# Moving the message sums between two sets of picks, and the addition of x behind the variance

## The chip, the cores and the metric

The kernel runs on one core of a Trainium2 chip. The metric is the device time in microseconds (us) of one execution. Inside the core five engines work from queues of their own and meet only at semaphores: TensorE (PE in the profile; PEld is its loading of weights), VectorE (DVE), ScalarE (ACT), GpSimd (POOL) and SyncE (SP), the last of which only issues transfers here.

## The reference

One layer of a graph network with a residual, on 100000 nodes of 96 numbers and 25000 edges whose target `dst` is sorted:

```python
h = jnp.maximum(_layernorm(x, axis=-1), 0.0)
concat = jnp.concatenate([h[src], h[dst], edge_attr], axis=-1)      # 25000 x 256
gates = jax.nn.sigmoid(concat @ W_e + b_e)
messages = jax.nn.softplus(concat @ W_n + b_n)
h_new = jax.ops.segment_sum(gates * messages, dst, num_segments=n)
edge_count = jnp.clip(segment_sum(ones, dst), 1.0, None)[:, None]
out = x + (h + h_new / edge_count)
```

## The kernel before

All five engines run the same loop of 49 steps (and a few steps of run-in and run-out), each with its own order of work written out by hand in a function `step(i)`. A step handles 2048 rows of x (16 rows in each of 128 partitions, "node rows") and 512 edges (4 tiles of 128). The engines work at different depths: in step i, DVE makes the statistics of node chunk i + 3, ACT and DVE normalize chunk i + 2, TensorE picks from chunk d = i + 1, edges k = i - 1 are transposed and multiplied, edges j = i - 2 go through the activations, and edges m = i - 3 are summed by target.

- TensorE, `step(i)` from L992. It first makes the **first set of picks** (`picks(d, 0, at)`, L1016): the rows of h that the sorted edges need are selected from node_out by multiplying with one-hot columns, 8 blocks, into the one tile `pick_ps` (L976). Their places come from 16 registers loaded at L967. It then transposes the gathered source rows (L1021) and the edge attributes (L1026), makes the **second set of picks** (L1030, again L976, with another register load), the **sums** (`sums(m)`, L1032, with L988 and L989: messages of equal target are added by a 0/1 matrix), and the final products of edges k (L1041 to L1043). Each set of picks waits for `pick_out`, ACT's copy of the set before out of `pick_ps`. The sums wait for `message_done`, `same_done` and `final_done`; the final products wait among others for `trans_out` and `attr_out`, ACT's copies of the transposes.
- ACT, `step(i)` from L498: sigmoid (L492), normalization of the gathered source rows (L508), the copy of the first picks into dst_t (L496), four node rows (L478), the copies of the transposes (L526, L528), the copy of the second picks (L496 again), then node rows mixed with the three activations of edges j (L540, L545, L550) and the logarithm and exponential of the variance (L484, L488). The last L478 of a step raises `node_norm_done`, for which the first picks of the next step wait.
- DVE, `step(i)` from L784: Newton steps for 1/sigma (L755 to L770), its share of node rows (L801, L806), the 0/1 matrices (L746, L749), the message (L739), statistics of node rows (L717), one-hot columns (L777), then **the addition of x** to the 16 normalized node rows of chunk d (L821, one operation over 128 x 1536, after both sets of picks have read them: it waits for `pick_done` 2d + 2), the statistics of the gathered rows (L826), counts (L722), inverse counts, `final` (L731) and the variance (L833 to L847), and the last two operations on the logarithms (L858, L861), which wait for ACT's L550.
- SP waits for L821 (`node_sum_done`) before it loads the next chunk of x (L304) and stores the finished one to out.
- POOL gathers source rows of x (L397) and adds `final` to rows of out (L411), four indirect transfers of each kind in a step. The latter wait for `final_done` and for the store of the chunk.

Of the kernel before, what the change touches and what calls it, by code (L numbers as in the profile page):

```python
# [52 lines left out]
def build(nc, x, src, dst, edge_attr, w_e, b_e, w_n, b_n, out, count_table, dst_pad, low_pad):  # L53
    ctx = ExitStack()
    with ctx:
# [544 lines left out]
        def _(dve):  # L600
# [183 lines left out]
            def step(i):  # L784
# [29 lines left out]
                for g in (0, 1) if i == -2 else (i + 3,):  # L814
                    if 0 < i + 3 and g < GROUPS:
                        one_hot(g)
                if runs_step(d):
                    wait(dve, node_norm_done, d + 1)
                    wait(dve, dve_norm_done, d + 1)
                    wait(dve, pick_done, 2 * d + 2)  # L820
                    nc.vector.tensor_tensor(node_out[d % NS][:, :, :], node_out[d % NS][:, :, :], node_x[d % NS][:, :, :],  # L821
                                            ALU.add).then_inc(node_sum_done, 1)
                if runs_step(i):
                    dve.wait_ge(gathered[i % NS], 16 * TB * (i // NS + 1))
                    for r in range(TB):
# [19 lines left out]
                if runs_rows(i):  # L845
                    wait(dve, diff_sq_done, i + 1 + LEAD)
                    nc.vector.scalar_tensor_tensor(out=var96[:, :], in0=diff_sq[:, :], scalar=D / 4.0, in1=sq_sum[:, :],  # L847
                                                   op0=ALU.mult, op1=ALU.add).then_inc(var_done, 1)
                if last_rows(i):
                    newton(i, None)  # L850
                    counts(m)
                    inverse_counts(m)
                    rows_to_write(m)
# [101 lines left out]
        def _(pe):  # L955
# [36 lines left out]
            def step(i):  # L992
                k, d, m = i - 1, i - 2 + LEAD, i - 3
                if i == 0:
                    pe.wait_ge(rows_f_done, 3)
                    nc.tensor.transpose(cols_ps[2][:, 0:P], index_rows_f[:, 2, 0, :], ident[:, :])
                    nc.tensor.transpose(cols_ps[2][:, P:TILES], index_rows_f[0:TILES - P, 2, 1, :],
                                        ident[0:TILES - P, 0:TILES - P]).then_inc(cols_done, 1)
                if i == 1:
                    pe.wait_ge(cols_read, 2)  # L1000
                    pe.wait_ge(weights_loaded, 16 * 10)
                    pe.wait_ge(ones_done, 6 + NM)
                if i == 2:
                    pe.wait_ge(violations_done, 1)
                    nc.tensor.matmul(total_ps, ones[:, :], violations[:, :], start=True, stop=True).then_inc(violations_summed, 1)
                if i == 3:
                    pe.wait_ge(flag_done, 1)
                if runs_step(d):
                    if d == 0:
                        pe.wait_ge(place_loaded, 16)  # L1010
                        pe.wait_ge(ones_done, 2)
                    at = places_of(2 * d)
                    wait(pe, node_norm_done, d + 1)
                    wait(pe, dve_norm_done, d + 1)
                    wait(pe, onehot_done, d + 2)
                    picks(d, 0, at)  # L1016
                if runs_step(k):
                    wait(pe, edge_norm_done, k + 1)
                    wait(pe, trans_out, k)
                    for t in range(TB):  # L1020
                        last = nc.tensor.transpose(trans_ps[0:D, t, :], src_h[k % 2][:, t, :], ident[:, :])  # L1021
                    last.then_inc(trans_done, 1)
                    pe.wait_ge(attr_loaded[k % NS], 16 * (k // NS + 1) + (16 if k == STEPS - 1 else 0))
                    wait(pe, attr_out, k)
                    for h in range(2):
                        last = nc.tensor.transpose(attr_ps[:, h, :],  # L1026
                                                   attr[k % NS][:, 2 * h:2 * h + 2, :].rearrange("p t f -> p (t f)"), ident[:, :])
                    last.then_inc(attr_trans_done, 1)
                if runs_step(d):
                    picks(d, 1, places_of(2 * d + 1))  # L1030
                if runs_step(m) and not ends(i, 1):
                    sums(m)  # L1032
                if runs_step(k):
                    wait(pe, softplus_done, k - 1)
                    wait(pe, trans_out, k + 1)
                    wait(pe, attr_out, k + 1)
                    wait(pe, pick_out, 2 * min(k + 2, STEPS))
                    for t in range(TB):
                        e = (k * TB + t) * P
                        z = z_ps[k % 2][:, t, 0:2 * D]  # L1040
                        nc.tensor.matmul(z, src_t[0:D + 1, t, :], w_src[0:D + 1, :], start=True, stop=False)  # L1041
                        nc.tensor.matmul(z, dst_t[0:D, e:e + P], w_dst[0:D, :], start=False, stop=False)  # L1042
                        last = nc.tensor.matmul(z, attr_t[:, t // 2, :], w_attr[t % 2][:, :], start=False, stop=True)  # L1043
                    last.then_inc(z_done, 1)
                if ends(i, 0):
                    sums(i - 2)
# [57 lines left out]
```

## Time and profile before

| | us |
|---|---|
| runs, median of 3 | 749.42 (746.96 to 753.84) |
| profiled execution, its own time | 752.55 |
| its span in the profile | 750.8 |
| busy: TensorE, DVE, ACT, POOL | 565.8, 552.5, 525.5, 542.9 |
| mean granted TensorE clock | 0.86 of full speed |
| share of the chain that ended last: PE, ACT, issue, DVE | 48%, 20%, 14%, 7% |

No engine is busy for more than three quarters of the span. A wait in the profile is put down to what came last by its records; "issue" is time for which they show no releaser, and "remote" stands for a releaser that they don't know.

### The profile page before, as it was taken

The numbers are of one execution on the slowest core, as the hardware profiler recorded it, in microseconds if no ns is written. First come the engines' busy times: TensorE is split into PE (matmuls) and PEld (weight loads), VectorE is DVE, ScalarE is ACT, GpSimd is POOL, SyncE is SP. The second block draws the span as 40 slices with busy tenths as digits, with TensorE's granted clock in tenths as the row PEclk, the third lists the DMA queues.
The fourth block names the chain that finished last, engine by engine and source line by source line (L and its number), as shares of the span: only waits on it lengthen the run. The fifth ranks groups of instructions, "written<-read, shape, count | busy, mean of one in ns | idle before, by whom it ended". The sixth has DMA issues, their size and how long they took to land.

```text
span 750.8 us, 14670 instructions
## 1 busy us (share of the span) xinstructions
PE 565.8 (75%) x3832; PEld 537.4 (72%) x3832; DVE 552.5 (74%) x2226; ACT 525.5 (70%) x1330; POOL 542.9 (72%) x404
## 2 busy tenths in 40 slices
PE   1046578888898898888887888889869778788870
PEld 0046577788788788788777887878769778778760
DVE  5766687877877787788787787787787969776550
ACT  0056677778788787786887877878868879688540
POOL 3502238888888888888888888888887878887585
PEclk9999888977987987897898898798897979889885
DMA  7435677978979879888688797897896978867442
GB/s 194 93 80 127 168 166 152 221 153 170 208 140 199 183 156 202 160 182 200 136 201 182 148 209 161 171 210 139 195 188 137 235 143 180 192 95 145 71 49 16
DMA packets 278376, 119.40 MB, mean 159 GB/s; under 512 B 261583, under 2 KB 268824, under 8 KB 278296
## 3 DMA queue, kind: packets, MB, share of 16 engines
q1 hardware_dynamic: 228366, 83.61, 46.4%
q0 software_dynamic: 34576, 18.40, 19.7%
q10 hardware_dynamic: 15354, 16.44, 8.7%
q8 instruction: 35, 0.57, 0.3%
q14 instruction: 45, 0.37, 0.1%
HBM read 71.36 MB, written 48.20 MB: 159 GB/s over the span
## 4 chain that ended last, share of the span: by engine, by line
PE 48%; ACT 20%; issue 14%; DVE 7%; ACTq 4%; POOL 3%; another core or an unknown queue 2%; DMA 1%; POOLq 0%; DVEq 0%
PE pick_ps L976 20%; ACT node_out L478 10%; PE sums_ps L988 6%; PE sums_ps L989 6%; PE z_ps L1041 5%; PE z_ps L1042 4%; PE z_ps L1043 4%; POOL out L411 3%; ACTq L322 3%; PE trans_ps L1021 2%; ACT log1p L550 2%; ACT log1p L545 2%; ACT log1p L540 2%; ACT src_h L508 1%
## 5 line engine op out<-in xcount | busy, mean ns | idle before, releaser
L411 POOL DMA_INDIRECT out<-final,scatter_idx x196 | 314.3, 1604 | 89.0 <-issue 57.3
L397 POOL DMA_INDIRECT edge_x<-in_x,src_idx x196 | 226.3, 1154 | 102.0 <-issue 59.2
L976 PE MATMUL pick_ps<-onehot,node_out 128*96 x1568 | 188.6, 285 | 140.5 <-issue 71.0
L976 PEld LDWEIGHTS pick_ps<-onehot,node_out 128*96 128x96 f32 x1568 | 175.4, 197 | 163.5 <-issue 163.2
L478 ACT ACTIVATE node_out<-node_x,shift,rstd 128x96 f32<-128x96 f32 x637 | 260.8, 457 | 20.6 <-DVE onehot L777 20.6
L821 DVE TENSOR_TENSOR node_out<-node_out,node_x 128x1536 f32<-128x1536 f32 x49 | 86.3, 1760 | 108.3 <-PE pick_ps L976 98.1
L496 ACT ACTIVATE dst_t<-pick_ps 96x336 f32 x98 | 43.8, 447 | 145.8 <-PE pick_ps L976 79.2
L717 DVE BATCH_NORM_STATS2 stats<-node_x 128x6 f32<-128x96 f32 x784 | 143.0, 246 | 1.3 <-issue 1.1
L1041 PE MATMUL z_ps<-w_src,src_t 97*128 97x192 f32 x392 | 106.9, 356 | 0.0
L1042 PE MATMUL z_ps<-w_dst,dst_t 96*128 96x192 f32 x392 | 101.7, 342 | 0.0
L988 PE MATMUL sums_ps<-messages,same 128*128 128x97 f32 x392 | 98.9, 343 | 3.7 <-DVE messages L739 3.7
L1043 PE MATMUL z_ps<-w_attr,attr_t 128*128 128x192 f32 x392 | 101.1, 340 | 0.0
L989 PE MATMUL sums_ps<-messages,same_prev 128*128 128x97 f32 x392 | 97.1, 338 | 0.0
L988 PEld LDWEIGHTS sums_ps<-messages,same 128*128 128x128 f32 x392 | 80.6, 254 | 3.9 <-DVE messages L739 3.9
L989 PEld LDWEIGHTS sums_ps<-messages,same_prev 128*128 128x128 f32 x392 | 80.6, 255 | 0.0
L508 ACT ACTIVATE src_h<-edge_x,shift,rstd 128x96 f32<-128x96 f32 x196 | 74.9, 453 | 1.7 <-DVE shift L770 1.7
L1041 PEld LDWEIGHTS z_ps<-w_src,src_t 97*128 97x128 f32 x392 | 75.5, 214 | 0.1
L1042 PEld LDWEIGHTS z_ps<-w_dst,dst_t 96*128 96x128 f32 x392 | 75.3, 205 | 0.0
L1043 PEld LDWEIGHTS z_ps<-w_attr,attr_t 128*128 128x128 f32 x392 | 73.8, 201 | 0.0
L801 DVE TENSOR_SCALAR node_out<-node_x,rstd,shift 128x96 f32<-128x96 f32 x147 | 39.9, 343 | 2.3 <-DVE shift L770 0.5
L550 ACT ACTIVATE log1p<-log1p 128x768 f32<-128x768 f32 x49 | 40.9, 835 | 0.1
L545 ACT ACTIVATE log1p<-log1p 128x768 f32<-128x768 f32 x49 | 40.9, 835 | 0.1
(117 smaller groups left out, 589.4 us busy)
## 6 DMA issues: line engine op xcount, KB each, us to landing
node_x<-in_x SPq DMA_DIRECT2D x48, 768.0 KB
out<-node_out SPq DMA_DIRECT2D x48, 768.0 KB
dst_across<-dst_pad ACTq DMA_DIRECT2D x49, 256.0 KB
attr<-in_edge_attr SPq DMA_DIRECT2D x48, 128.0 KB
edge_x<-in_x,src_idx POOLq DMA_INDIRECT x196
out<-final,scatter_idx POOLq DMA_INDIRECT x196
low_across<-low_pad ACTq DMA_DIRECT2D x47, 64.0 KB
node_x<-in_x SPq DMA_DIRECT2D x1, 624.0 KB
```

The costliest lines, as they stand in the source:

```text
L397: nc.gpsimd.indirect_dma_start(out=edge_x[i % NS][:, t, :], out_offset=None, in_=x, in_offset=bass.IndirectOffsetOnAxis(ap=src_idx[:, i * ...
L411: nc.gpsimd.indirect_dma_start(out=out, in_=final[j % FINALS][:, t, :], in_offset=None, out_offset=bass.IndirectOffsetOnAxis(ap=scatter_id ...
L478: last = nc.scalar.activation(node_out[n % NS][:, r, :], node_x[n % NS][:, r, :], ACT.Relu, bias=shift[us][:, c:c + 1], scale=rstd[us][:, ...
L508: last = nc.scalar.activation(src_h[k % 2][:, t, :], edge_x[u][:, t, :], ACT.Relu, bias=shift[u][:, t:t + 1], scale=rstd[u][:, t:t + 1])
L717: last = nc.vector.bn_stats(stats[:, TB + r, :], node_x[c % NS][:, r, :])
L821: nc.vector.tensor_tensor(node_out[d % NS][:, :, :], node_out[d % NS][:, :, :], node_x[d % NS][:, :, :], ALU.add).then_inc(node_sum_done, 1)
L976: last = nc.tensor.matmul(pick_ps[0:D, bass.ds(to[b], WINDOW)], node_out[d % NS][:, h * BLOCKS + b, :], onehot[:, bass.ds(of[b], WINDOW)], ...
L988: nc.tensor.matmul(sum_ps[:, t, :], same[:, t, :], cur, start=True, stop=False)
L989: last = nc.tensor.matmul(sum_ps[:, t, :], same_prev[:, t, :], prev, start=False, stop=True)
L1041: nc.tensor.matmul(z, src_t[0:D + 1, t, :], w_src[0:D + 1, :], start=True, stop=False)
L1042: nc.tensor.matmul(z, dst_t[0:D, e:e + P], w_dst[0:D, :], start=False, stop=False)
L1043: last = nc.tensor.matmul(z, attr_t[:, t // 2, :], w_attr[t % 2][:, :], start=False, stop=True)
```

## The change

In TensorE's step the sums of edges m are made before the second set of picks instead of after it. In DVE's step the addition of x to the node rows is made after the variance instead of before the statistics of the gathered rows. The operations, their operands and their waits stay as they are. The waits move with them: what stands behind L821 in DVE's queue before (L826 to L847) now stands ahead of it.

```diff
@@ DVE, step(i)
-                if runs_step(d):
-                    wait(dve, node_norm_done, d + 1)
-                    wait(dve, dve_norm_done, d + 1)
-                    wait(dve, pick_done, 2 * d + 2)
-                    nc.vector.tensor_tensor(node_out[d % NS][:, :, :], node_out[d % NS][:, :, :], node_x[d % NS][:, :, :],
-                                            ALU.add).then_inc(node_sum_done, 1)
                 if runs_step(i):
                     dve.wait_ge(gathered[i % NS], 16 * TB * (i // NS + 1))
...
                     nc.vector.scalar_tensor_tensor(out=var96[:, :], in0=diff_sq[:, :], scalar=D / 4.0, in1=sq_sum[:, :],
                                                    op0=ALU.mult, op1=ALU.add).then_inc(var_done, 1)
+                if runs_step(d):
+                    wait(dve, node_norm_done, d + 1)
+                    wait(dve, dve_norm_done, d + 1)
+                    wait(dve, pick_done, 2 * d + 2)
+                    nc.vector.tensor_tensor(node_out[d % NS][:, :, :], node_out[d % NS][:, :, :], node_x[d % NS][:, :, :],
+                                            ALU.add).then_inc(node_sum_done, 1)
                 if last_rows(i):
@@ TensorE, step(i)
                     last.then_inc(attr_trans_done, 1)
+                if runs_step(m) and not ends(i, 1):
+                    sums(m)
                 if runs_step(d):
                     picks(d, 1, places_of(2 * d + 1))
-                if runs_step(m) and not ends(i, 1):
-                    sums(m)
```

## Rows read from the trace of the kernel before

**Rows 1.** Waits: engine, line, releaser: us in total, times, longest us.

```profile
DVE node_out L821 <- PE pick_ps L976: 98.1, 41, 7.4
ACT dst_t L496 <- PE pick_ps L976: 79.2, 55, 3.5
```

**Rows 2.** ACT's timeline (start us, us, line, idle before), first copies, steps 4 and 48.

```profile
98.87 0.45 ACT L496 ACTIVATE dst_t<-pick_ps 96x336 f32 x1 [3.50 <-PE pick_ps L976]
...
697.11 0.45 ACT L496 ACTIVATE dst_t<-pick_ps 96x336 f32 x1 [3.29 <-remote]
```

**Rows 3.** ACT's timeline, one step.

```profile
413.32 0.45 ACT L496 ACTIVATE dst_t<-pick_ps 96x336 f32 x1
...
418.55 0.82 ACT L478 ACTIVATE node_out<-node_x,shift,rstd 128x96 f32<-128x96 f32 x2
...
419.93 1.53 ACT L508 ACTIVATE src_h<-edge_x,shift,rstd 128x96 f32<-128x96 f32 x4
423.74 0.45 ACT L496 ACTIVATE dst_t<-pick_ps 96x336 f32 x1 [2.29 <-remote]
...
426.00 0.37 ACT L528 ACTIVATE attr_t<-attr_ps 128x256 f32<-128x256 f32 x1
427.28 0.45 ACT L496 ACTIVATE dst_t<-pick_ps 96x336 f32 x1 [0.91 <-PE pick_ps L976]
```

**Rows 4.** TensorE's timeline, the same stretch.

```profile
413.03 0.41 PE L988 MATMUL sums_ps<-messages,same 128*128 128x97 f32 x2
...
414.85 0.52 PE L1041 MATMUL z_ps<-w_src,src_t 97*128 97x192 f32 x2
...
418.47 0.49 PE L1043 MATMUL z_ps<-w_attr,attr_t 128*128 128x192 f32 x2
419.51 1.57 PE L976 MATMUL pick_ps<-onehot,node_out 128*96 x16 [0.56 <-issue]
421.51 0.64 PE L1021 MATMUL trans_ps<-ident,src_h 128*96 128x128 f32 x4 [0.43 <-ACT src_h L508]
421.99 0.38 PE L1026 MATMUL attr_ps<-ident,attr 128*128 128x128 f32 x2
424.34 2.82 PE L976 MATMUL pick_ps<-onehot,node_out 128*96 x16 [1.97 <-issue]
426.95 0.69 PE L988 MATMUL sums_ps<-messages,same 128*128 128x97 f32 x2
...
430.42 0.90 PE L1041 MATMUL z_ps<-w_src,src_t 97*128 97x192 f32 x2
```

**Rows 5.** Windows: stretch, its us, busy us (count) by engine, granted clock, DMA, GB/s.

```profile
424.00:424.50 0.50, 0.16 (x1) 0.17 (x2) 0.50 (x3) 0.50 (x3) 0.50 (x1) 0.78 1.27 244
...
434.50:435.00 0.50, 0.50 (x5) 0.50 (x4) 0.39 (x2) 0.50 (x2) 0.50 (x1) 0.98 1.27 313
```

**Rows 6.** TensorE's timeline at two other places.

```profile
67.72 1.06 PE L1021 MATMUL trans_ps<-ident,src_h 128*96 128x128 f32 x4
69.08 1.66 PE L976 MATMUL pick_ps<-onehot,node_out 128*96 x16
...
588.77 1.57 PE L976 MATMUL pick_ps<-onehot,node_out 128*96 x16 [0.99 <-ACT dst_t L496]
```

**Rows 7.** DVE's timeline, the step of rows 3.

```profile
421.53 0.56 DVE L739 TENSOR_TENSOR messages<-log1p 128x384 f32<-128x384 f32 x1
...
424.10 0.47 DVE L777 TENSOR_SCALAR onehot<-low_across,lane 128x512 f32<-128x512 uint8 x1
427.29 1.76 DVE L821 TENSOR_TENSOR node_out<-node_out,node_x 128x1536 f32<-128x1536 f32 x1 [2.72 <-PE pick_ps L976]
```

**Rows 8.** Line L967, TensorE's register loads: ns min/median/max.

```profile
L967 PEldq TENSOR_LOAD <-dst_t x98: 1101/1109/3537, 28.5 to 694.0; - x98
```

**Rows 9.** Timelines of ACT and POOL: two waits outside the steady part.

```profile
63.20 0.22 ACT L484 ACTIVATE log_var<-var 128x20 f32<-128x20 f32 x1 [1.08 <-DVE var L847]
...
706.06 1.55 POOL L411 DMA_INDIRECT out<-final,scatter_idx  x1 [6.21 <-DVE final L731]
```

## The prediction

> **What bounds the kernel now.** I read the waits first. The two largest that the diff touches are DVE's wait of 98.1 us before L821 for the second set of picks, and ACT's wait of 79.2 us before L496 for picks [rows 1]. Both are averages over a loop, so I then followed one step of the loop.
>
> The loop's pace: the first copy of step 4 starts at 98.87 and that of step 48 at 697.11 [rows 2], so 44 steps take 598.24 us, 13.60 us each. The 152 us outside them are start and tail.
>
> In the timeline of ACT [rows 3] I count from N, the end of the last L478, 418.55 + 0.82 = 419.37. L508 ends at 421.46 = N + 2.09. The first copy (L496) starts at N + 4.37 after an idle time put down to "remote". L528 ends at 426.37 = N + 7.00, which is when ACT is ready for the second copy; that one starts at N + 7.91, 0.91 us late, for the picks. From a second copy to the next N it is 419.37 - 413.32 = 6.05 us. So ACT needs 7.00 + 6.05 = 13.05 us for a step in which nobody is late at the second copy.
>
> TensorE's timeline [rows 4] says who is late. The first picks start at N + 0.14, the transposes at N + 2.14, as soon as L508 is done, and end with L1026 at N + 3.00. Then TensorE has nothing it may do for 1.97 us: the second picks overwrite pick_ps and wait for ACT's first copy (423.74 + 0.45 = 424.19, picks at 424.34). In that gap the granted clock falls from 1.00 to 0.50, that is from 2.4 to 1.2 GHz (0.78 is the mean of the half microsecond in which it falls), and it comes back only near 434.5 [rows 5]. The second picks then take 2.82 instead of 1.57 us, and the sums 3.47 (426.95 to 430.42) instead of 1.82 (413.03 to 414.85). Of the 44 steps 21 have such slow second picks, roughly every other one; the mean of 13.60 is one over slow and fast steps. Three engines are tied in one circle here, none is busy throughout.
>
> **The change, part by part.** No instruction is added or removed, 49 times in each case one group is moved.
>
> *Sums before the second picks (16 matmul records, L988 and L989).* They need `message_done`: L739 ends at 421.53 + 0.56 = N + 2.72 [rows 7]. TensorE's transposes let the next group start at about N + 2.85 (the records of neighbours overlap by some 0.16). So the sums start at once and fill N + 2.85 to N + 4.67, the idle gap. That is the good half. The second picks now come behind them in TensorE's queue, and behind the picks' own register load: L967 takes 1.10 us at the least and 3.54 at the most, 1.11 in the median [rows 8]. Where nothing else held them, second picks started 0.99 us after the transposes (at 588.77) [rows 6]; the bounds for the gap after the sums are thus 0 (load wholly under the sums, which are longer than the transposes) and 1.0. I take 0.5, since the queue reaches the load before the sums are through. Second picks: N + 5.3 to N + 6.9 at the full clock, copy at N + 7.0. ACT is ready at N + 7.00. So with the full clock a step costs 13.05 us (13.0 to 13.5 with the bounds), 0.55 less than today's mean.
>
> What is late next is TensorE's idle time. The final products (L1041 to L1043) need `attr_out`, that is the end of L528 at N + 7.0, and take 4.11 us (414.85 to 418.47 + 0.49 = 418.96): they end at N + 11.2, and the next picks can't start before the next N + 0.14 = N + 13.2. Before the change the sums stood in this stretch and the gap in front of the first picks was 0.56 us [rows 4]. Now it is 2.0 us in every step that runs at the full clock: the idle time has been moved from in front of the second picks to in front of the first ones. I expect the clock to fall there as it did at the old place.
>
> And there it costs more. From N on TensorE's whole chain is on the path that sets the next N: first picks 2.6 (start to start of the next group, 424.34 to 426.95), transposes 1.36 (67.72 to 69.08, where they ran at the low clock [rows 6], against 0.70), sums 3.47, second picks 1.4 if the clock has returned and 2.6 if not, 0.1 to the copy, then 6.05. Sum from N + 0.14: 15.1 or 16.3 us. The register load is then under the slow sums. The low clock lasted some 10 us at the place shown [rows 5], enough for the whole chain, but it need not start with the first picks nor last as long; I take 15.6 for such a step, bounds 14.8 (1.2 us of picks and some sums escape) and 16.4.
>
> How often? After a step in which the final products too ran slow they end late and fill the gap, so the next step should be a fast one; and the gap of 0.99 at 588.77 did not bring the clock down [rows 6]. Today one step in two falls with a gap of 1.97. I take 2 in 5: 0.6 x 13.05 + 0.4 x 15.6 = 14.07 us, 0.47 more than 13.60. Over 44 steps: +20.7 us.
>
> The Trainium skill, TensorE: Matmul & The Clock Gate, section "Loop structure matters more than you think", says that the clock is kept where groups of matmuls follow each other back to back and lost where each group stands behind a long wait. Rows 4 and 5 agree, with a gap of 1.97. The page speaks against this change in so far as it puts such a gap into every fast step; taken strictly every step would be a slow one, which is the third rival below.
>
> *L821 behind the variance.* DVE reaches the end of the one-hot at 424.10 + 0.47 = N + 5.2 [rows 7]. It then does the edge statistics, counts, `final` and variance without waiting for the second picks (the sums are done at N + 4.8), an estimated 2 us of mostly small operations (L826 to L847), and takes up L821 at about N + 7.1, with the picks just done: the wait of 98.1 us mostly goes, and the 1.76 us of L821 move behind them. What is behind L821 now: the two operations at L858 and L861, which wait for ACT's L550 anyway, three activations and two node rows behind the second copy. So L821, done at N + 8.8, is hidden, price 0. SP's load of x and store of a chunk, which wait for L821, go out at N + 8.8; in the step shown it was 427.29 + 1.76 - 419.37 = N + 9.7. If L821 did delay L858 and through it ACT's next sigmoid, 1.76 us a step would be the most that it costs.
>
> Gains outside the steady part: ACT's wait for the variance, 1.08 us in the early steps [rows 9], goes in two of them (and 0.26 us in each slow step, which is beside the longer chain): -2.5 us. At the end POOL waited 6.21 us for `final` until 706.06 [rows 9], and from there its scatters run nearly back to back to the end. `final` of that step will come about 5 us sooner: -5 (bounds 0 and -6.2).
>
> Sum on the profiled execution's own 752.55 us (span 750.8): +20.7 - 2.5 - 5 = +13, 765.7. The median of the runs is 749.42, 0.4% below it, so 762 us in its terms.
>
> **The rivals.**
>
> *The clock stays up.* For it: the new gap has 4 us of final products ahead of it, the old one only the short group of transposes. Against it: both are 2 us. Every step then takes 13.05 to 13.3: -0.3 to -0.55 x 44 = -13 to -24, less 7.5 for start and tail: about 722 in the median's terms. This is the rival on the other side; it decides from the point at which fewer than 1 step in 5 falls (0.55 / 2.55 = 0.22).
>
> *It falls in about one step of four.* Mean step 13.65, as now, and only start and tail gain: 744.
>
> *It falls in every step.* 44 x (15.3 - 13.6) = +75, less 7.5: 814. Against it: slow final products close the gap after a long low stretch.
>
> *The sums don't start in the gap*, since the messages come late. L739 ends only 0.13 us before they are wanted. Were they 0.5 us late, a step would be 0.5 longer, +22 on the first rival: again 744; I count it with the second one.
>
> **How the numbers follow.** Two runs of this kernel can be told apart from about 1%. Chances: my forecast 0.42, the clock stays up 0.20, one in four 0.23, every step 0.12, and 0.03 for something else. Around the forecast the fraction of slow steps (0.3 to 0.55) and their length (14.8 to 16.4) give 750 to 790. The range for 8 in 10 takes in the one-in-four case, most of the first rival (720 and up) and stops short of the last one: 720 to 800. Faster by over 1% (below 742): the first rival and less than half of the second, 0.30. Slower (above 757): 0.50. Same: 0.20.
>
> **What would show each step right or wrong.** In the profile after: the sums start right behind the transposes, about 2.9 us behind the last L478, and the gap before the second picks is under 1 us; the gap in front of the first picks is near 2 us in steps at the full clock. Fast steps take 13.0 to 13.3 us from one first copy to the next, slow ones 15 to 16.3, and in the slow ones the first picks, transposes and sums all run at the low clock; the mean granted clock is no higher than today's. DVE's wait before L821 (its new line) falls far below 98 us, ACT's wait for picks grows. I am wrong if the granted clock is near 1 throughout (then the kernel is faster), if the register load adds a full microsecond to the fast steps, or if L821 delays L858 so that ACT waits at its first activation of a step.

## The result

The changed kernel takes 831.07 us (median of 4 runs, 829.23 to 837.01), the kernel before 748.19 (745.71 to 753.84): 1.111 times as long, 95% interval 1.104 to 1.118. I had predicted 762, with a range of 720 to 800. The sign was the likelier one of mine; the size lies outside the range, and the rival nearest to it (the clock falls in every step, 814) names a cause to which experiment 12 leaves 17 of the 83 us. The profiled execution took 837.01 us, against 752.55 before.

From the page of the profile after: the busy times, GpSimd in the 40 slices of the span (tenths), and the shares of the chain that ended last:

```profile
PE 570.1 (68%) x3832; PEld 549.6 (66%) x3832; DVE 550.1 (66%) x2226; ACT 523.2 (63%) x1330; POOL 554.8 (66%) x404
...
POOL 4403088768678668688586786768768767766675
...
ACT 39%; PE 26%; another core or an unknown queue 14%; issue 7%; ACTq 5%; DVE 3%; POOL 2%; DMA 2%; POOLq 0%; SPq 0%; DVEq 0%
```

No engine has much more to do: the busy time of GpSimd and that of the weight loads rose by 12 us each, the others by less. 14% of the chain, some 117 us, is a wait whose releaser the profile can't name; before it was 2%. The waits of after (line numbers have moved: L847 is the addition that was L821) say where:

```profile
ACT dst_t L496 <- remote: 123.5, 22, 6.8
POOL out L411 <- DVE final L731: 105.8, 24, 19.5
ACT dst_t L496 <- PE pick_ps L976: 104.5, 61, 5.8
DVE node_out L847 <- remote: 67.4, 19, 4.8
...
DVE node_out L847 <- PE pick_ps L976: 15.7, 20, 2.9
```

DVE's wait for picks fell from 98.1 to 15.7 us [rows 1], as predicted, but 67.4 us of "remote" stand beside it, and ScalarE's copies have 123.5 of the same. GpSimd, of which I had said next to nothing, waits 105.8 us for `final` in front of its scatters, and 30.5 before.

The copies of a few steps, in ScalarE's timeline of after (start us, us, line, idle before; first and second copy in turn):

```profile
409.58 0.45 ACT L496 ACTIVATE dst_t<-pick_ps 96x336 f32 x1 [0.38 <-PE pick_ps L976]
415.75 0.45 ACT L496 ACTIVATE dst_t<-pick_ps 96x336 f32 x1 [3.55 <-remote]
...
433.99 0.45 ACT L496 ACTIVATE dst_t<-pick_ps 96x336 f32 x1 [6.48 <-remote]
443.12 0.45 ACT L496 ACTIVATE dst_t<-pick_ps 96x336 f32 x1 [1.17 <-PE pick_ps L976]
...
447.89 0.45 ACT L496 ACTIVATE dst_t<-pick_ps 96x336 f32 x1 [2.15 <-PE pick_ps L976]
456.36 0.45 ACT L496 ACTIVATE dst_t<-pick_ps 96x336 f32 x1 [0.32 <-issue]
...
464.79 0.45 ACT L496 ACTIVATE dst_t<-pick_ps 96x336 f32 x1 [5.80 <-remote]
```

From second copy to second copy it is 18.24, 13.90 and 16.90 us. Before, the late copy was the first of a step [rows 3]; now it is the second. TensorE's timeline of the last of these steps (lines of the final products left out but for the last):

```profile
454.08 1.84 PE L976 MATMUL pick_ps<-onehot,node_out 128*96 x16 [2.34 <-ACT node_out L478]
456.09 1.09 PE L1021 MATMUL trans_ps<-ident,src_h 128*96 128x128 f32 x4 [0.17 <-ACT src_h L508]
...
457.40 0.58 PE L988 MATMUL sums_ps<-messages,same 128*128 128x97 f32 x2
...
459.75 1.50 PE L976 MATMUL pick_ps<-onehot,node_out 128*96 x16
...
464.73 0.49 PE L1043 MATMUL z_ps<-w_attr,attr_t 128*128 128x192 f32 x2
```

and DVE's and GpSimd's of the same step:

```profile
462.03 0.17 DVE L841 SCALAR_TENSOR_TENSOR var<-diff_sq,sq_sum 128x20 f32<-128x20 f32 x1
464.80 1.76 DVE L847 TENSOR_TENSOR node_out<-node_out,node_x 128x1536 f32<-128x1536 f32 x1 [2.60 <-remote]
...
457.48 1.02 POOL L397 DMA_INDIRECT edge_x<-in_x,src_idx  x1 [0.30 <-issue]
...
461.54 0.95 POOL L397 DMA_INDIRECT edge_x<-in_x,src_idx  x1 [0.30 <-issue]
463.06 1.62 POOL L411 DMA_INDIRECT out<-final,scatter_idx  x1 [0.57 <-issue]
```

The second picks end at 459.75 + 1.50 = 461.25, and TensorE goes straight on to the final products. Both engines that wait for the picks, ScalarE at L496 and DVE at L847, start at 464.79 and 464.80: 3.54 us late, both at the same moment. So the picks are done and the signal that says so is late. I call this a late signal. Taken over the 44 steps from the fifth to the 48th, the second copy starts 0.12 us behind the last pick in a prompt step; it is over 0.5 us behind it in 24 steps, and the 44 delays sum to 83.8 us, against 6.7 before. (The first copies went the other way, from 68.5 to 23.0 us; part of their delay is only ScalarE being busy.) The step's mean has gone from 13.60 [rows 2] to 15.54 us (second copies at 117.57 and 785.97, 43 steps), which over 44 steps is 85 us: nearly the whole loss, and close to what the delays at the second copies grew by, 77 us. That agreement alone doesn't show that they are the cause.

### The profile page after: what moved, and what is told of

The parts are those of the page before. It is cut to its first block, busy times and chain, and to the rows that moved or that the text cites. A ratio compares the mean times of both kernels' runs of the same rounds, so it can differ in the third digit from the quotient of the medians.

```text
span 835.3 us, 14670 instructions
## 1 busy us (share of the span) xinstructions
PE 570.1 (68%) x3832; PEld 549.6 (66%) x3832; DVE 550.1 (66%) x2226; ACT 523.2 (63%) x1330; POOL 554.8 (66%) x404
## 4 chain that ended last, share of the span: by engine, by line
ACT 39%; PE 26%; another core or an unknown queue 14%; issue 7%; ACTq 5%; DVE 3%; POOL 2%; DMA 2%; POOLq 0%; SPq 0%; DVEq 0%
ACT node_out L478 21%; PE pick_ps L976 15%; ACT log1p L550 4%; ACT log1p L545 4%; ACT log1p L540 4%; PE sums_ps L988 4%; PE sums_ps L989 4%; ACTq L322 3%; PE trans_ps L1021 3%; POOL out L411 2%; ACTq L567 2%; ACT src_h L508 1%; ACT dst_t L496 1%; ACT src_t L526 1%
## 5 line engine op out<-in xcount | busy, mean ns | idle before, releaser
L411 POOL DMA_INDIRECT out<-final,scatter_idx x196 | 354.7, 1810 | 163.4 <-DVE final L731 105.8
L976 PE MATMUL pick_ps<-onehot,node_out 128*96 x1568 | 195.9, 293 | 226.8 <-ACT node_out L478 215.9
L976 PEld LDWEIGHTS pick_ps<-onehot,node_out 128*96 128x96 f32 x1568 | 184.2, 206 | 241.8 <-issue 241.8
L397 POOL DMA_INDIRECT edge_x<-in_x,src_idx x196 | 197.8, 1009 | 100.3 <-issue 59.1
L496 ACT ACTIVATE dst_t<-pick_ps 96x336 f32 x98 | 43.9, 447 | 240.8 <-remote 123.5
L847 DVE TENSOR_TENSOR node_out<-node_out,node_x 128x1536 f32<-128x1536 f32 x49 | 86.1, 1757 | 83.3 <-remote 67.4
L1041 PE MATMUL z_ps<-w_src,src_t 97*128 97x192 f32 x392 | 100.9, 339 | 0.7 <-ACT attr_t L528 0.7
L989 PE MATMUL sums_ps<-messages,same_prev 128*128 128x97 f32 x392 | 91.8, 323 | 0.0
L858 DVE SCALAR_TENSOR_TENSOR log1p<-z_ps,log1p 128x384 f32<-128x384 f32 x49 | 27.3, 558 | 83.4 <-ACT log1p L550 83.4
L508 ACT ACTIVATE src_h<-edge_x,shift,rstd 128x96 f32<-128x96 f32 x196 | 74.9, 453 | 1.2 <-DVE shift L770 1.2
L1041 PEld LDWEIGHTS z_ps<-w_src,src_t 97*128 97x128 f32 x392 | 68.7, 195 | 0.9 <-issue 0.8
L1021 PE MATMUL trans_ps<-ident,src_h 128*96 128x128 f32 x196 | 50.4, 410 | 5.3 <-ACT src_h L508 5.2
L722 DVE TENSOR_SCALAR count<-sums_ps 128x4 f32<-128x4 f32 x49 | 7.8, 160 | 55.3 <-PE sums_ps L989 47.2
```

The lines of the kernel that those rows point to most:

```text
L397: nc.gpsimd.indirect_dma_start(out=edge_x[i % NS][:, t, :], out_offset=None, in_=x, in_offset=bass.IndirectOffsetOnAxis(ap=src_idx[:, i * ...
L411: nc.gpsimd.indirect_dma_start(out=out, in_=final[j % FINALS][:, t, :], in_offset=None, out_offset=bass.IndirectOffsetOnAxis(ap=scatter_id ...
L508: last = nc.scalar.activation(src_h[k % 2][:, t, :], edge_x[u][:, t, :], ACT.Relu, bias=shift[u][:, t:t + 1], scale=rstd[u][:, t:t + 1])
L976: last = nc.tensor.matmul(pick_ps[0:D, bass.ds(to[b], WINDOW)], node_out[d % NS][:, h * BLOCKS + b, :], onehot[:, bass.ds(of[b], WINDOW)], ...
L989: last = nc.tensor.matmul(sum_ps[:, t, :], same_prev[:, t, :], prev, start=False, stop=True)
```

## The experiments

Each was timed against the kernel before on its own chip. Experiments 1 to 4 and 9 to 12 ran on one chip, 5 to 8 on a second, 13 to 16 on a third, 17 and 18 on a fourth; the medians of before beside 1 to 4, 5 to 8, 9 to 12, 13 to 16 and 17 to 18 were 748.1, 740.2, 748.8, 745.9 and 748.4 us. Where chips differ, the ratios to before are what can be compared.

**1 and 2: each part alone.** First the addition moved and the sums left behind the second picks; then the sums moved and L821 left where it was:

```diff
--- the changed kernel
+++ e1
-                if runs_step(m) and not ends(i, 1):
-                    sums(m)
                 if runs_step(d):
                     picks(d, 1, places_of(2 * d + 1))
+                if runs_step(m) and not ends(i, 1):
+                    sums(m)
--- the kernel before
+++ e2
+                if runs_step(m) and not ends(i, 1):
+                    sums(m)
                 if runs_step(d):
                     picks(d, 1, places_of(2 * d + 1))
-                if runs_step(m) and not ends(i, 1):
-                    sums(m)
```

> Only the DVE part of the change: x is added to the node rows behind the variance, TensorE still picks before it sums. Theory A (the loss is TensorE's completion signals arriving late at the second picks, because the sums now stand in front of them): the late signal stays on the first picks, where most of it is hidden, so this kernel stays within 2% of before, 740 to 763 us. Theory B (the loss comes from the later addition, which starts the x load and the store of the rows later): most of the 83 us is here, 800 to 831 us. Theory C (both needed): under 763 here and under 763 for TensorE alone.

Measured: 770.49 us, 22 over before, but only roughly: its four executions (758.94 to 780.14) lie 11 to 32 us over it.

> Only the TensorE part: the sums stand between transposes and second picks, the addition stays ahead of the edge statistics. Theory A (late signals at the second picks): the second copy on ScalarE starts 1.5 to 5 us behind the last second pick in about half of the steps and the time is 800 to 831 us. Theory B (late addition): 745 to 765 us. Theory of the clock, as in the prediction: first picks slow in many steps, no late signals at the second, 755 to 775 us.

Measured: 758.60 us, 1.010 times before (1.006 to 1.014). All three theories on the DVE part missed: alone it costs some 22 us. For the TensorE part the theory of the clock gave the right time (+10.5 us) and no late signals at the second picks, and there are none: all 44 second copies start 0.12 us behind the last pick. The two parts alone add up to some 33 us (21 to 43 by the spread); together they cost 83. So some 50 us (40 to 62) belong to neither part but to the two together.

**3 and 5: GpSimd's halves taken out of the changed kernel.** The loop over the four scatters, or over the four gathers, runs only in the first four steps, and the waits on their semaphores are cut to match:

```diff
-                    for t in range(TB):
+                    for t in range(TB if j < FINALS else 0):      # e3; e5: "if i < NS", at the gathers
```

> The changed kernel with GpSimd's scatter-add left out from the fifth edge tile on (the output lacks those messages; everything else runs, with its waits). Theory A1 (the signals of TensorE come late while GpSimd issues scatters): the delay behind the second picks falls under 0.3 us in nearly all steps, step about 13.0 us, total 700 to 740 us. Theory A2 (late for a reason other than GpSimd's indirect DMAs): delay stays near 2 us a step, total 800 to 831 us. Theory P (GpSimd is the bound, since its scatters now wait for the sums): total also falls to 700 to 740, but then the delays stay.

> The changed kernel with GpSimd's gathers left out from the fifth edge tile on (edge rows keep the first tiles' values, so the output is not the reference's; all else runs). Removing the scatters took the time from 831 to 748 us and the late signals with them. Theory A1 (scatters alone make TensorE's signals late): the delay behind the second picks stays over 1 us a step and the time over 770 us. Theory P (GpSimd's row, gathers and scatters together, is the bound and everything late follows from its being full): without 5.2 us of gathers a step it has slack, delays shrink under 0.5 us a step and the time falls to 740 to 760 us, as it did without scatters.

Measured: 748.30 us without the scatters, 1.001 times before (0.997 to 1.005), and 751.15 without the gathers, 1.018 times before (1.014 to 1.022). The waits at the copies, first without the scatters, then without the gathers, where no "remote" is left among the listed waits:

```profile
ACT dst_t L496 <- PE pick_ps L976: 141.0, 70, 4.9
...
ACT dst_t L496 <- remote: 20.2, 4, 7.6
```

```profile
ACT dst_t L496 <- PE pick_ps L976: 146.4, 68, 4.9
...
ACT dst_t L496 <- issue: 9.0, 23, 0.6
```

Taking out the scatters takes back the whole loss, taking out the gathers all but 11 us of it, and either nearly all late signals. A1 (scatters alone) fell with the second of them, A2 with the first; P had the fall right in both, but without scatters neither its size nor the delays. The circle of the other three engines needs 13.7 us a step (e5), no better than the kernel before.

**4, 6 and 7: other waits on GpSimd.** In the changed kernel its scatters wait for `final`. I tried one more wait there, and the opposite: each scatter one step later (LAG 6), so that `final` is long there.

```diff
                     wait(pool, final_done, j + 1)
+                    if j + 1 + LEAD < STEPS:                      # e4
+                        wait(pool, pick_done, 2 * (j + 1 + LEAD) + 2)
```

> The changed kernel with one more wait: GpSimd starts the four scatters of a step only when the second picks of that step have been signalled. In the changed kernel the signal came 3.5 to 5 us late in the steps in which a scatter started meanwhile, and at most 1.8 us late where none did. Theory A1 (a scatter issued during the delay prolongs it): the delay falls under 2 us everywhere, the long steps of 17 to 18 us shrink to about 15 us, total 770 to 805 us. Theory P (GpSimd bound): each wait adds to GpSimd's row, total 831 to 870 us.

> The changed kernel with LAG 6 in place of 5: GpSimd writes the rows of a step one step later, so the scatters never have to wait for the row division of the same step. Nothing is left out. In the changed kernel GpSimd idles 2.04 us a step there. Theory P (the loss is GpSimd's waiting in front of its scatters): that idle time goes, the step falls from 15.7 to about 13.7 us and the time to 745 to 765 us. Theory A1 (the loss is TensorE's late signals, whatever GpSimd waits for): the signals are still late, 800 to 831 us.

> The kernel before with LAG 6. GpSimd idles 0.37 us ahead of its scatters in the kernel before, hardly more than the 0.30 us between any two of its transfers. Theory P (GpSimd has no slack before, and waits for nothing): no change, 740 to 755 us. Theory A1 says the same unless the phase of the scatters against the picks matters: then it moves by over 10 us, either way.

Measured: e4 833.48 us (1.111 times before), e6 852.38 us (1.155 times before), e7 740.39 us (1.001 times). In e4 the alternation of long and short steps is gone, nearly all take 15.1 to 16.1 us, and the second copies are mostly 1 to 2.5 us late. GpSimd's and ScalarE's rows of one step there:

```profile
425.40 0.94 POOL L397 DMA_INDIRECT edge_x<-in_x,src_idx  x1 [0.30 <-issue]
428.08 2.48 POOL L413 DMA_INDIRECT out<-final,scatter_idx  x1 [1.73 <-PE pick_ps L978]
...
427.30 0.45 ACT L498 ACTIVATE dst_t<-pick_ps 96x336 f32 x1 [3.79 <-PE pick_ps L978]
```

The signal comes 0.9 us behind the end of the last gather (426.34), and only then do scatters start: a circle of eight transfers (from 412.54 to 426.34 in this step, 13.8 us) and 1.7 us of waiting, 15.5 in all. P had the time right. A1 had the time wrong, and of the delays only that the longest would shrink: from 5.0 to 3.3 us, still over 2 us in 13 of 44 steps, 1.6 us on average in place of 1.9. In e6 the simple theory P fell: GpSimd no longer had to wait for the same step's `final`, waited elsewhere instead (for L508 in front of its gathers, 120.1 us in 25 waits, 41.1 in the changed kernel), and the time rose, above what either theory had given. So taking away the wait for the same step's `final` does not help. What remained to be tried was the place of its transfers in the step.

**8: the kernel before without scatters.**

> The kernel before without the scatters from the fifth tile on (the output lacks those messages). Theory P (the kernel before is bound by GpSimd's 13.6 us a step): the step falls to what the other engines need, 12.3 to 12.8 us, and the time to 680 to 710 us; the changed kernel without scatters took 748, so the change would then cost about 50 us with GpSimd out of it. Theory of the clock (both kernels differ by the clock alone once GpSimd is out): 735 to 755 us.

Measured: 735.70 us, 0.996 times before (0.993 to 0.999). So GpSimd's row is not the only bound of the kernel before; with half of it gone, the circle of the other engines takes the same 13.6 us. Late first copies remain (57.0 us of "remote" at L496, 25 times), with gathers alone.

**9 and 13: the place of the gathers.** In the kernel before GpSimd gathers the edge rows of step i from about the second copy of step i-2 on: four gathers and four scatters follow each other with 0.30 us between two and take as long as the step. In the changed kernel the gathers stand beside the second picks (rows above: gathers from 457.48 to 462.49, picks to 461.25). One wait forbids that:

```diff
                     wait(pool, edge_norm_done, i - NS + 1)
+                    wait(pool, pick_done, 2 * i)                  # e9; e13: only "if i < 12"
                     pool.sem_inc(pool_go, 1)
```

> The changed kernel with one more wait: GpSimd gathers edge tile i only once the second picks of step i-2 have been signalled. That is where these gathers start by themselves in the kernel before (0.4 to 1.2 us behind the second copy) and with the TensorE part alone; in the changed kernel they start some 6 us ahead of it and run beside the second picks. Theory F (TensorE's signals come late only where gathers and the scatters behind them stand beside the picks, so it is the phase of GpSimd's row that the addition's new place has shifted): the delay behind the second picks falls from 1.95 to under 0.5 us a step, the step to 13.8 us, the time to 750 to 775 us. Theory G (the phase is a consequence, not the cause): 825 us or more, since GpSimd is given one more wait.

> The changed kernel with the gathers' wait for the second picks only for the first 12 edge tiles; from the 13th on nothing differs from the changed kernel. Theory H (two stable orders: GpSimd's gathers either start with the second copy or end beside the second picks, and each keeps itself going; the start decides which): the good order holds to the end, 745 to 765 us. Theory F2 (the wait has to hold the gathers back in every step): the late signals come back soon after the 12th tile, 800 to 825 us.

Measured: e9 745.98 us, 0.996 times before (0.993 to 0.999); e13 744.24 us, 0.999 (0.995 to 1.002). The whole loss is gone, and it stays away when the wait is there for the first 12 tiles only. GpSimd's timeline in e9 (lines moved by one), one set of gathers and the scatters behind it:

```profile
368.20 1.49 POOL L398 DMA_INDIRECT edge_x<-in_x,src_idx  x1 [0.30 <-issue]
...
372.52 0.94 POOL L398 DMA_INDIRECT edge_x<-in_x,src_idx  x1 [0.30 <-issue]
373.77 1.73 POOL L412 DMA_INDIRECT out<-final,scatter_idx  x1 [0.30 <-issue]
...
379.73 1.55 POOL L412 DMA_INDIRECT out<-final,scatter_idx  x1 [0.30 <-issue]
```

and ScalarE's copies beside them:

```profile
366.76 0.44 ACT L497 ACTIVATE dst_t<-pick_ps 96x336 f32 x1
377.38 0.45 ACT L497 ACTIVATE dst_t<-pick_ps 96x336 f32 x1 [2.62 <-remote]
380.01 0.45 ACT L497 ACTIVATE dst_t<-pick_ps 96x336 f32 x1
```

GpSimd does not pause here, gathers start 1.4 us behind a second copy, and scatters stand beside both sets of picks. The late signal has gone back to the first copy, where it was before the change. There it seems to cost nothing: e13, in nearly the same order, had no "remote" at L498 at all in its profiled execution and took 0.999 times before, e9 0.996. But they ran on different chips, and what keeps late first copies from costing time is not shown. The added wait itself rarely holds GpSimd: up to 330 us it pauses in front of its gathers five times at the start (25.70 to 4.25 us) and three times by 2.4 us later on, then four more times by 2.4 us; in e13 it does not pause again once the wait has ended. It sets the order once, and the order keeps itself.

**14: the addition's place in the right order.** The DVE part alone, with the wait of e9.

> The DVE part alone with the gathers' wait. The DVE part alone took 770 us, with steps of 11.5 to 16.5 us and GpSimd idle ahead of its scatters in 11 of 40 steps. Theory H (its loss too is GpSimd's row out of phase): within 1% of before, 740 to 756 us. Theory B (the later addition itself costs about 0.5 us a step): stays at 762 to 775 us.

Measured: 740.50 us, 0.993 times before (0.989 to 0.997). So the addition behind the variance costs nothing by itself, as the prediction had it. That its 22 us alone were GpSimd's order too is likely but not shown: experiment 1 ran on another chip, and on this one late signals were rare whatever the kernel (see 16).

**10, 11, 12 and 15: the clock.** Extra matmuls of the identity into a spare corner of PSUM, in the idle time that the granted clock falls in.

```diff
                     last.then_inc(z_done, 1)
+                    if i >= 4:                                    # e10, e12, e15: behind the final products
+                        for _ in range(8):
+                            nc.tensor.matmul(attr_ps[:, 2, :], ident[:, :], ident[:, :], start=True, stop=True)
```

In e11 nine narrower ones (112 columns) stand behind the transposes, behind a wait for `final_done`.

> The TensorE part alone, and 8 extra matmuls of the identity into a spare corner of PSUM behind the z products of each step (about 1.8 us), where TensorE would stand idle 2.3 us in front of the first picks. In the TensorE part alone steps with both sets of picks fast take 12.3 us, those with slow ones 13.3 to 15.8, 13.8 us on average. Theory of the clock (the idle time in front of the first picks costs what the prediction said): 12.3 to 12.9 us a step, 690 to 720 us. Without an effect of the clock: 755 to 765 us.

> The kernel before with 9 extra matmuls of the identity behind the transposes, in the idle time in front of the second picks where the changed kernel has its sums. Theory of the clock: the second picks are fast in all steps, half of which had them 1.25 us slower: 0.6 us a step, 720 to 735 us. Theory that the late first copy sets the step whatever the picks cost: 740 to 755 us.

> The changed kernel with the same 8 extra matmuls in front of the first picks. In the changed kernel the first picks are slow in 26 of 43 steps. Theory A (late signals at the second picks set the step): the clock rises over 0.9 and the time stays over 800 us. Theory of the clock: 750 to 790 us.

> The changed kernel with the gathers' wait in all steps and 8 extra matmuls in front of the first picks: a candidate for a kernel that beats both. Theory of the clock: its two steps of 15.6 us in ten go, 13.69 us a step becomes 13.2, 720 to 735 us. Theory S (with the clock up the late first copy takes over, as it did with the TensorE part alone, at 13.65 us a step): 740 to 750 us.

Measured: e10 (TensorE part alone) 755.70 us, e11 (before) 736.62, e12 (changed) 814.13, e15 (changed, with the wait of e9) 735.91, against 748.75 and, for e15, 745.86 of before. The theories of the clock missed in e10 and e12; in e11 and e15 the time lies between the two forecasts. The mean granted clock went from 0.848 to 0.972 in e10, from 0.86 to 0.965 in e11 and from 0.834 to 0.902 in e12. In e10 nearly every step took 13.6 to 13.9 us, although the clock stayed up. ScalarE's rows there:

```profile
357.67 0.45 ACT L496 ACTIVATE dst_t<-pick_ps 96x336 f32 x1 [2.42 <-remote]
360.84 0.45 ACT L496 ACTIVATE dst_t<-pick_ps 96x336 f32 x1 [0.55 <-issue]
371.31 0.45 ACT L496 ACTIVATE dst_t<-pick_ps 96x336 f32 x1 [2.58 <-remote]
```

The first copy is over 0.5 us late in 40 of 44 steps and comes 10.47 us behind the second copy of the step before. GpSimd has no pause in the loop either, and its eight transfers take 13.7 us as well; which of the two sets the step is not shown. So raising the clock this far gains 3 us in e10, 17 in the changed kernel, where it rose least, and 12 in the kernel before (0.986 times it, 0.978 to 0.993). e15 is the fastest form of the change, 0.988 times before (0.984 to 0.992), and no better than e11, which needs no change of order.

**16 and 18: pushing the order over.** GpSimd's scatters held up until the second picks of the following step: in the kernel before at its 13th and 29th set, in e13's kernel at its 25th.

```diff
                     wait(pool, final_done, j + 1)
+                    if j in (12, 28):                             # e16; e18: j == 24
+                        wait(pool, pick_done, 2 * (j + 2 + LEAD) + 2)
```

> The kernel before with GpSimd held up twice, once at its 13th and once at its 29th set of scatters, until the second picks of the following step are signalled (some 6.5 us each). Theory H in its strong form (the kernel before has the bad order too, and only its start keeps it out): after the 13th tile the steps grow to 15 us and more with late signals at the second picks, 780 us or more. Weak form (only the changed kernel can stay in the bad order; before returns to the good one in a step or two): under 765 us.

> The changed kernel put into the good order by the gathers' wait over the first 12 tiles, and then held up once, at the 25th set of scatters, until the second picks of the following step are signalled. Without the hold-up it kept the good order to the end (744 us). Theory H in its two-sided form (the changed kernel keeps whichever order it is in): from there on it runs in the bad order, 21 steps of about 15.7 in place of 13.7 us, 775 to 795 us. One-sided (it falls back into the good order): 744 to 757 us.

Measured: e16 745.27 us, 0.999 times before (0.995 to 1.002); e18 754.17 us, 1.007 (1.004 to 1.010), its 11 executions from 749.76 to 784.7. The time of e16 says nothing on theory H, since its trace shows no push: neither of the two sets of scatters had to wait.

```profile
268.09 2.39 POOL L413 DMA_INDIRECT out<-final,scatter_idx  x1 [0.30 <-issue]
...
492.86 1.62 POOL L413 DMA_INDIRECT out<-final,scatter_idx  x1 [0.30 <-issue]
```

What it does show is a limit of the reading above. In this execution of the kernel before, 32 of 44 second sets of picks ended beside GpSimd's last two gathers or the scatter behind them, and no copy was over 0.5 us behind. In the changed kernel 24 sets end there, and all 24 copies are late, 3.37 us on average. One such set of e16, in GpSimd's, TensorE's and ScalarE's timelines:

```profile
418.99 1.62 POOL L413 DMA_INDIRECT out<-final,scatter_idx  x1 [0.30 <-issue]
...
418.66 1.91 PE L978 MATMUL pick_ps<-onehot,node_out 128*96 x16
...
420.70 0.45 ACT L498 ACTIVATE dst_t<-pick_ps 96x336 f32 x1 [0.37 <-PE pick_ps L978]
```

The place of the transfers alone is thus not enough. All four profiles of that chip (e13 to e16) have prompt signals; the changed kernel was not run there without an added wait, so whether it would lose its 83 us on that chip is open. In e14, e15 and e16 the loop also runs ahead of GpSimd: 62 to 72 us of the span follow the first copy of step 48, 54 in the kernel before.

In e18 the push took hold. The changed kernel got over it, within four steps (7.82 us of pause at 433.92, prompt second copies again from 481.05 on); but the profiled execution of e18, one of its slower ones with 764.89 us, went over to the bad order by itself later. ScalarE's copies there:

```profile
578.59 0.45 ACT L500 ACTIVATE dst_t<-pick_ps 96x336 f32 x1 [2.88 <-PE pick_ps L980]
...
611.03 0.45 ACT L500 ACTIVATE dst_t<-pick_ps 96x336 f32 x1 [6.81 <-remote]
...
639.87 0.45 ACT L500 ACTIVATE dst_t<-pick_ps 96x336 f32 x1 [4.09 <-remote]
```

From 593.29 to the end of the loop its steps take 15.3 us on average. For the changed kernel neither form of theory H is right as I wrote it: the push did not do it, and yet the kernel can leave the good order, and in this execution it did not come back.

**17: the changed kernel once more**, beside e18.

> The changed kernel as it is, once more, beside the next run on the same chip. The four kernels run last showed late first copies of only 0.4 us where earlier profiles of the same order showed 1.5 to 2.4, with the same times. If the late signals at the second picks are what costs the changed kernel its 83 us, they are here again, 1.5 to 2.5 us a step, and the time is 820 to 840 us. If they vary with the chip and cost nothing, they are small and the time stays 820 to 840 us, and the loss must be GpSimd's idle time of 2 us a step alone.

Measured: 830.92 us, 1.110 times before (1.104 to 1.116), with 111.4 us of "remote" at L496 and a second copy 1.68 us behind the last pick on average (1.90 in the first profile). The loss and the late signals repeat. On this same chip the kernel of e18, with its wait over the first 12 tiles and in spite of its push, took 754 us.

## Why the prediction was wrong, point by point

*What bounds the kernel.* "Three engines are tied in one circle here, none is busy throughout." This is the sentence from which the error comes. The circle is there, but GpSimd runs beside it with only 0.30 us between two transfers, in 13.6 us for the eight of a step. I had looked at GpSimd's waits at start and tail only [rows 9] and not at its row in the loop. The experiments point to two limits of equal height: without scatters the kernel before is only 0.4% faster.

*Sums in the idle gap.* Right. In a fast step of the TensorE part alone they start at N + 2.79 and the second copy comes at N + 6.27 (from 344.55 to 350.82), where I had 7.0; the register load costs nothing there, its lower bound.

*The idle time moves in front of the first picks and the clock falls there.* Right as a mechanism: 2.34 us in front of the picks at 454.08, and the clock is down by the transposes. These windows of the changed kernel show it (columns as in rows 5):

```profile
456.00:456.50 0.50, 0.41 (x2) 0.40 (x3) 0.47 (x2) 0.18 (x2) 0.50 (x1) 0.50 1.23 300
460.00:460.50 0.50, 0.50 (x9) 0.50 (x8) 0.00 (x0) 0.00 (x0) 0.21 (x1) 1.00 0.08 8
```

It comes back before the second picks, sooner than I had bounded it. The size was wrong. My term for the loop was +20.7 us; in the TensorE part alone the 44 steps from first copy to first copy (98.47 to 705.00) take 606.53 us, +8.3. A long step there takes 15.2 to 15.8 us, as I had said, but only 9 of 44 are that long (from second copy to second copy), and the one behind is mostly 12.3 us, shorter than my fast step of 13.05. That this kernel's +10.5 us lies near my +13 is luck: my sum was +20.7 less 7.5 at the start and end, and this kernel has +8.3 in the loop and hardly anything outside it. With the clock kept up, the same kernel gains only 3 us and stays at 13.7 us a step. A mean of 13.0 us from step 4 to 48 is met once, in e15, and there 68 us of the span follow the first copy of step 48 in place of 54.

*L821 behind the variance: price 0.* This is the step that failed: the runs show some 22 us for it alone, 83 together with the sums, and 83.8 us of delay at the second copies. Its own time is hidden, as said (e14: 0.993 times before), and DVE waits less. What the sum left out is that the operations which overtake it include `final` (L731), for which GpSimd's scatters wait. In the changed kernel `final` no longer stands behind the addition, and so not behind the second picks. GpSimd's first scatter, in the kernel before and in the changed one:

```profile
106.05 1.63 POOL L411 DMA_INDIRECT out<-final,scatter_idx  x1 [21.04 <-DVE final L731]
```

```profile
102.77 2.57 POOL L411 DMA_INDIRECT out<-final,scatter_idx  x1 [19.51 <-DVE final L731]
```

The second copies of that step start at 101.54 and 102.06. So the first scatter comes 4.5 us behind it before, 0.7 us behind it after, and the eight transfers that follow put the next gathers beside second picks instead of behind them. That the order decides is shown where late signals occur at all: one wait added to the changed kernel gives 746 us (e9) on a chip on which other forms of it took 833 and 814 (e4, e12), and on another chip the kernel with the wait over the first 12 tiles took 754 us beside 831 without it (e18, e17). e16 shows the limit: on its chip the same place of the gathers did no harm to the kernel before. That it is this first scatter which sets the order is argued from these two rows and from the early wait of e13 being enough; I did not move `final` alone.

*Why 831 and not 770.* With the sums ahead of them, the second picks end with the final products queued right behind and nothing else of ScalarE's to do; every late signal there goes into the step in full. The DVE part alone has the picks earlier and late signals mostly elsewhere. This is read from the traces, not tested by itself.

*Start and tail.* Predicted -2.5 and -5 us. From first copies, as I had counted, the start gained 2.6 us (step 4 at 96.31 in place of 98.87), as said, and the tail nothing: 55.7 in place of 55.4 us from the first copy of step 48 to the end. The 6.21 us of GpSimd's wait at the end turned into others of the same kind.

*The rivals.* None of them was it. All four were made of the clock and of late messages. A rival on GpSimd was missing, although rows 3 already showed 2.29 us of "remote" that I used as a given and did not ask about. In the profile before, 20 of 44 first sets of picks end beside GpSimd's last two gathers or the scatter behind them, and all 20 copies are late.

## What to carry to other kernels

A transfer queue that runs wall to wall can be a limit of the loop even if no chain runs through it: when an operation that releases its transfers is overtaken by, or overtakes, another one, work out where in the step its transfers will stand, not only how long the moved operation takes. Two parts of a change that cost 22 and 10 us apart can cost 83 together; time them apart and together. And where a loop can run in more than one order, one wait in the first steps can be worth more than any saving in the steady state: here it was worth 85 us.

## What the runs showed of the hardware that I had not expected

TensorE's signals can reach the engines that wait for them microseconds late, while TensorE itself goes on: 3.54 us at 464.79 in the changed kernel, 2.4 to 2.6 us at the first copies of e9 and e10. The traces tie it to a place in GpSimd's row: from the start of a step's third gather to the end of the first scatter behind the gathers (or of the last gather, where GpSimd then pauses). From the fifth to the 48th step of the 13 profiles that have all of GpSimd's work, those of e13 to e16 left out, 373 sets of picks ended in that stretch, and in 363 cases the copy started over 0.5 us behind them, 2.46 us on average. Elsewhere in the step it was 147 of 771, 0.34 us on average, and that includes copies for which ScalarE was only busy. With either half of GpSimd's work taken out of the changed kernel the late signals are nearly gone (e3, e5); with gathers alone in the kernel before they remain (e8).

In the four profiles of e13 to e16, all of one chip, 140 sets of picks ended in the same stretch and the copy was over 0.5 us behind in 31, 0.30 us on average, hardly more often than elsewhere in the step there (32 of 212). So the lateness needs GpSimd's transfers and something else that this chip, or those executions, did not have. What holds the signals back is open, and so is why late first copies cost nothing in e9 (2.2 us late on average, 0.996 times before).
